# Cross-attention and 8-bit FFN on one core: both stages' quantisation factors moved from VectorE to GpSimd

## What is computed

```python
x = x + xattn(layernorm(x), ctx, mask)            # attention over 64 context rows
def _act_quant(x):                                # one factor for each row
    scale = 127.0 / clip(max(abs(x), axis=-1), 0.0001, None)
    return clip(round(x * scale), -128, 127) / scale
def _linear_bit(x, w, g):                         # w becomes ternary
    return einsum('bsd,od->bso', _act_quant(g * rmsnorm(x)), _ternary_quant(w))
n = layernorm(x)
h = silu(_linear_bit(n, w1, g1)) * _linear_bit(n, w2, g2)     # 512 -> 2048
x = x + _linear_bit(h, w3, g3)                                # 2048 -> 512
```

## Time and profile before

| what | value |
|---|---|
| median of 3 runs | 471.03 us (470.67 to 472.04) |
| the profiled execution | 472.33 us, of which the span from first to last instruction is 470.5 us |
| TensorE busy | 409.9 us (87%) |
| VectorE busy | 407.1 us (87%) |
| ScalarE busy | 339.5 us (72%) |
| GpSimd busy | 341.3 us (73%) |

### The profile page before, as it was taken

One profiled execution on the slowest core, in us unless ns is written; L12 is line 12 of the kernel. 1 busy time (PEld: TensorE's weight loads), 2 busy tenths in 40 slices (PEclk: granted clock), 3 DMA queues, 4 the chain that ended last, 5 costly groups with the idle time before them and its releaser, 6 DMA issues. The chain is left out here.

```text
span 470.5 us, 8445 instructions
## 1 busy us (share of the span) xinstructions
PE 409.9 (87%) x1966; PEld 197.5 (42%) x1966; DVE 407.1 (87%) x927; ACT 339.5 (72%) x607; POOL 341.3 (73%) x539
## 2 busy tenths in 40 slices
PE   8326644899999999999999999999999999999995
PEld 8102412344644464446434543445444634334432
DVE  3799576889899999999999999999999999999662
ACT  1585446986798769886988788878886796666552
POOL 0267858787777787788788787778777877878650
PEclk9756795899999999999999999999999999999998
DMA  7999901545557455745574466447654444444431
GB/s 270 396 366 421 312 16 22 135 90 114 139 148 173 90 114 143 179 88 115 165 178 89 111 182 163 90 111 189 139 129 111 91 88 91 86 94 91 90 69 45
DMA packets 110504, 67.45 MB, mean 143 GB/s; under 512 B 100752, under 2 KB 100880, under 8 KB 106768
## 3 DMA queue, kind: packets, MB, share of 16 engines
q1 hardware_dynamic: 110480, 67.19, 53.9%
HBM read 34.14 MB, written 8.39 MB: 90 GB/s over the span
## 5 line engine op out<-in xcount | busy, mean ns | idle before, releaser
L521 POOL TENSOR_TENSOR stageB<-stageB,g3b 128x512 f32<-128x512 f32 x128 | 163.8, 1285 | 46.2 <-DVE stageB L907 45.3
L1163 PE MATMUL S<-W2q,q12T 128*128 128x512 f16 x512 | 134.5, 386 | 8.9 <-DVE stageB L907 6.2
L1163 PE MATMUL S<-W1q,q12T 128*128 128x512 f16 x512 | 135.3, 388 | 0.0
L693 ACT ACTIVATE sg<-S,asc 128x512 f32<-128x512 f32 x128 | 87.5, 683 | 54.1 <-PE S L1163 49.3
L1191 PE MATMUL DN<-W3q,stageB 128*128 128x512 f16 x512 | 118.7, 386 | 7.3 <-DMA stageB<-stageB 7.3
L907 DVE TENSOR_TENSOR stageB<-sg,S 128x512 f32<-128x512 f32 x128 | 86.7, 677 | 19.9 <-ACT sg L693 10.5
L913 DVE TENSOR_REDUCE hm<-stageB 128x1 f32<-128x512 f32 x128 | 86.5, 677 | 0.2 <-POOL stageB L521 0.2
L1163 PEld LDWEIGHTS S<-W2q,q12T 128*128 128x128 f16 x512 | 49.5, 99 | 75.3 <-DVE stageB L907 13.9
L1191 PEld LDWEIGHTS DN<-W3q,stageB 128*128 128x128 f16 x512 | 49.8, 99 | 70.3 <-issue 10.8
L1163 PEld LDWEIGHTS S<-W1q,q12T 128*128 128x128 f16 x512 | 49.8, 100 | 66.3 <-issue 10.1
L685 ACT ACTIVATE stageB<-stageB,hf 128x1024 f16<-128x1024 f32 x64 | 69.8, 1140 | 4.8 <-DVE hf L933 4.8
(11 more groups left out here) (112 smaller groups left out, 430.7 us busy)
## 6 DMA issues: line engine op xcount, KB each, us to landing
xTs<-in_xT SPq DMA_DIRECT2D x8, 1024.0 KB, 7.0
X<-in_x SPq DMA_DIRECT2D x8, 1024.0 KB, 6.0
out_x<-X SPq DMA_DIRECT2D x32, 256.0 KB, 2.9
X<-in_w1T SPq DMA_DIRECT2D x4, 1024.0 KB, 12.5
stageB<-in_w2T SPq DMA_DIRECT2D x4, 1024.0 KB, 20.4
X<-in_w3T SPq DMA_DIRECT2D x4, 1024.0 KB, 9.2
ctxr<-in_ctx SPq DMA_DIRECT2D x16, 128.0 KB, 3.1
ctxc<-in_ctx SPq DMA_DIRECT2D x8, 128.0 KB, 3.9
```

The costliest lines, as they stand in the source:

```text
L521: nc.gpsimd.tensor_tensor(gh[q][:, part], hp[:, part], g3b[:, part], ALU.mult).then_inc(s_gh_made, 1)
L693: nc.scalar.activation(sg[n % 2][:, :], S1[n % 2][:, :], ACT.Silu, scale=asc[z][:, 0:1])\
L1163: mm = nc.tensor.matmul(bank[n % 2][:, :], q12T[q][:, i * KD + k, :], w[:, n, k, :], start=(k == 0), stop=(k == KD - 1))
```

## The change

Four things change. VectorE keeps, for each stage, the plain row maximum and one reciprocal of it: `ar = 1/am` right behind `am`, and `hr = 1/hm1` right behind `hm1`. The rest of both factors is computed on GpSimd with a minimum in place of the clip: `127 * k / max(m*k, 1e-4)` is written as a constant times `min(1e-4 / m, k)`. GpSimd also makes the scale `hsc`, which gets two buffers, while `ha` has one. In stage A the two columns of `aa` and of `af` are one instruction each, where VectorE used two.

The first part of the diff is GpSimd's new functions, the second its slot, the last two VectorE's functions and slot.

```diff
+            def stage_a_factor(t, z):
+                pool.wait_ge(s_a_am, t + 1)
+                pool.wait_ge(s_a_k, t + 1)
...
+                nc.gpsimd.tensor_scalar(aa[z][:, :], am[:, :], ak[:, :], ACT_MAX_FLOOR, ALU.mult, ALU.max)\
+                    .then_inc(s_a_max, 1)
...
+                pool.wait_ge(s_a_r, t + 1)
+                nc.gpsimd.tensor_scalar(af[:, :], ar[:, :], ACT_MAX_FLOOR, ak[:, :], ALU.mult, ALU.min).then_inc(s_a_f, 1)
             def quantize_12(t):
-                pool.wait_ge(s_a_f, 2 * (t + 1))
+                pool.wait_ge(s_a_f, t + 1)
             def stage_h_root(t, z):
...
+                nc.gpsimd.tensor_scalar(hkk[:, :], hk[:, :], asc[z][:, 1:2], QMAX * QUANTUM / ACT_MAX_FLOOR, ALU.mult, ALU.mult).then_inc(s_h_kk, 1)
+            def stage_h_factor(t):
+                pool.wait_ge(s_h_kk, t + 1)
+                pool.wait_ge(s_h_max, t + 1)
...
+                nc.gpsimd.tensor_scalar(ha[:, :], hm1[:, :], hkk[:, :], QMAX * QUANTUM, ALU.mult, ALU.max).then_inc(s_h_a, 1)
+                pool.wait_ge(s_h_r, t + 1)
...
+                nc.gpsimd.tensor_scalar(hf[:, :], hr[:, :], QMAX * QUANTUM, hkk[:, :], ALU.mult, ALU.min).then_inc(s_h_f, 1)
+            def worth_3(t, q):
...
+                nc.gpsimd.tensor_scalar(hsc[q][:, :], ha[:, :], wc[:, 2:3], ACT_MAX_FLOOR / (QMAX * QUANTUM), ALU.mult, ALU.mult).then_inc(s_h_sc, 1)
@@ GpSimd, slot @@
                     stage_h_root(t - 1, (j - 1) % NZ)
+                    stage_h_factor(t - 1)
+                    if not (first and j == 1):
+                        worth_3(t - 1, (j - 1) % 2)
                 if ahead:
                     stage_a_mean(t + 2, (j + 2) % TPB)
                 if not (last and j == TPB - 1):
+                    stage_a_factor(t + 1, (j + 1) % NZ)
                     quantize_12(t + 1)
@@ VectorE @@
             def stage_a_max(t):
...
+                dve.wait_ge(s_a_am, t + 1)
+                nc.vector.reciprocal(ar[:, :], am[:, :]).then_inc(s_a_r, 1)
             def stage_h_top(t):
...
+                nc.vector.reciprocal(hr[:, :], hm1[:, :]).then_inc(s_h_r, 1)
@@ VectorE, slot @@
                     stage_h_top(t - 1)
-                    if not early:
-                        stage_h_factor(t - 1, (j - 1) % NZ, (j - 1) % 2)
                 if ahead and not (first and j == 0):
                     stage_a_gain(t + 2)
...
-                    worth_3(t - 2, j % 2)
-                    result(t - 2)
+                    result(t - 2, j % 2)
...
-                if ahead:
-                    stage_a_factor(t + 2, (j + 2) % NZ)
```

More of the change, by code:

```diff
@@ L153, in bit_ffn_xattn @@
         hkk = sb("hkk", [P, 1])
-        ha = [sb(f"ha{i}", [P, 1]) for i in range(2)]
+        ha = sb("ha", [P, 1])
         hr = sb("hr", [P, 1])
         hf = sb("hf", [P, 1])
-        hsc = sb("hsc", [P, 1])
+        hsc = [sb(f"hsc{i}", [P, 1]) for i in range(2)]
         S1 = [ps(f"S1_{i}", [P, CH]) for i in range(2)]
@@ L879, in stage_a_max @@
                 dve.wait_ge(s_a_ga, 2 * (t + 1))
+                if later(t):
+                    dve.wait_ge(s_a_max, t)
                 nc.vector.tensor_reduce(am[:, :], ga[:, :, :], AX_X, ALU.max, apply_absolute_value=True)\
                     .then_inc(s_a_am, 1)
-            def stage_a_factor(t, q):
                 dve.wait_ge(s_a_am, t + 1)
[L886 to L899, removed]
+                if later(t):
+                    dve.wait_ge(s_a_f, t)
+                nc.vector.reciprocal(ar[:, :], am[:, :]).then_inc(s_a_r, 1)
             def gate(t, n):
@@ L918, in stage_h_top, with result @@
                 dve.wait_ge(s_gh_max, NCH * (t + 1))
+                if later(t):
+                    dve.wait_ge(s_h_a, t)
                 nc.vector.tensor_reduce(hm1[:, :], hm[:, :], AX_X, ALU.max).then_inc(s_h_max, 1)
[L921 to L925, removed]
                 dve.wait_ge(s_h_max, t + 1)
-                nc.vector.tensor_scalar(ha[q][:, :], hm1[:, :], hkk[:, :], ACT_MAX_FLOOR, ALU.mult, ALU.max).then_inc(s_h_a, 1)
-                dve.wait_ge(s_h_a, t + 1)
-                nc.vector.reciprocal(hr[:, :], ha[q][:, :]).then_inc(s_h_r, 1)
-                dve.wait_ge(s_h_r, t + 1)
                 if later(t):
-                    dve.wait_ge(s_c3_made, NHALF * t)
-                nc.vector.tensor_scalar(hf[:, :], hr[:, :], hkk[:, :], QMAX * QUANTUM, ALU.mult, ALU.mult)\
-                    .then_inc(s_h_f, 1)
-            def worth_3(t, q):
-                if later(t):
-                    dve.wait_ge(s_x2_made, t)
-                nc.vector.tensor_scalar(hsc[:, :], ha[q][:, :], wc[:, 2:3], None, ALU.mult).then_inc(s_h_sc, 1)
-            def result(t):
+                    dve.wait_ge(s_h_f, t)
+                nc.vector.reciprocal(hr[:, :], hm1[:, :]).then_inc(s_h_r, 1)
+            def result(t, q):
                 dve.wait_ge(s_down_ps, t + 1)
@@ L1053, in slot @@
                 if not early and j != 1:
-                    worth_3(t - 2, j % 2)
-                    result(t - 2)
+                    result(t - 2, j % 2)
                 if attn and j < 3:
                     stage_a_max(t + 2)
-                if first and j == 1:
-                    stage_h_factor(0, 0, 0)
                 gate(t, 2)
```

42 lines of the change are left out of this document (29 added, 13 removed).

## The result

The changed kernel took 533.83 us (median of 4 runs, 532.84 to 535.06), the kernel before 471.53 us on the same chip (4 runs, 470.67 to 472.22). The ratio is 1.132, with a 95% interval of 1.128 to 1.136: 62 us slower, where 24 were forecast.

The account below looks back on a forecast made before the run. VectorE's instruction list was taken as the period, TensorE close behind. Per slot 2.20 - 0.61 - 0.41 - 0.35 = +0.83 us, over 28 slots 23.2; with the ends +24.4 on 471.03, rounded up to 496 us; range 484 to 514.

Parts of the forecast that it names:

- the step named as the one on which the forecast rests: Each slot: `c12` now stands behind `ha`, which waits for `hm1`, so `ga` starts 2.20 us later.
- `ga`'s pair takes 1.42 us: Sign in the changed profile: a pair of `ga` takes 1.42 us everywhere, 0.35 us saved for each.
- VectorE's busy share fell: Sign in the changed profile: VectorE's busy share falls below 80% in the loop.
- the waits of `gain_3` for gates: Sign in the changed profile: GpSimd's waits for gates ahead of `gain_3` shrink.
- `ha` follows `hm1` by 0.15 us: Sign in the changed profile: `ha` follows `hm1` by 0.2 us.
- the price of the small instructions in the trip: GpSimd between `hm1` and `ga`: five small instructions 1.05 us, `af` 0.43, within a trip of 3.12 us.
- the dearest: Upper bound: each small GpSimd instruction 0.37 us from start to start, trip 3.92 us, slot +1.63, 518 us.
- The savings: VectorE per slot: stage A 0.61 us, `hsc` 0.41, `ga` pair 0.35, against `ga` 2.20 later: +0.83 us.
- the rule: VectorE and GpSimd share a port pair; the first holds it, so `ga` right behind `c12` saves 0.35 us.
- Rival 1: GpSimd itself becomes the bound: 1.6 us more in a slot against 1.8 slack; about 511 us; chance 0.22.
- `hkk` costs nothing here: In the trip: `hk` ends 2 us before `hm1`, so `hkk` is covered; otherwise 0.35 us on top.
- The ends: Outside the loop: tile 1's slot 1.0 us, the kernel's end +0.2, first tiles' weight waits nothing; batch 7's slots 0, 1 +0.83 each.

Follow-up runs that it names:

- The wait alone: Plain-copy form of the kernel before, GpSimd only waiting for `hm1` of the tile before ahead of the codes `c12`, nothing moved: 483.27 us, ratio 1.025.
- codes first: Plain-copy form of the changed kernel, with `ha`, `hf` and `hsc` moved behind `c12`, `asc` and `asq` in GpSimd's list: 509.66 us, ratio 1.082.
- both remedies: Plain-copy form of the changed kernel, `ha`, `hf`, `hsc` moved behind `c12`, `asc`, `asq`, and two `ga` buffers: 501.48 us, ratio 1.062.
- eight fillers: Plain-copy form of the kernel before, with eight small GpSimd instructions that nobody needs added behind `asq` in each slot: 485.58 us, ratio 1.024.
- stage A alone: Plain-copy form of the kernel before, with only `aa` and `af` moved to GpSimd, stage H staying on VectorE: 476.69 us, ratio 1.009.
- stage H alone: Plain-copy form of the kernel before, with only `hkk`, `ha`, `hf` and `hsc` moved to GpSimd, `aa` and `af` on VectorE: 510.39 us, ratio 1.085.

## Why the prediction was right in kind and wrong in size

**Right.** Slower, and by the step named as the one on which the forecast rests: the codes behind `hm1`. The wait alone costs 13.6 us, and the changed profile shows the round trip in every slot. `ga`'s pair takes 1.42 us, VectorE's busy share fell (40.88 of 58.25 us), the waits of `gain_3` for gates went from 29.1 us in 240 to 1.8 us in 270, and `ha` follows `hm1` by 0.15 us where GpSimd is in time.

**The step that failed: the price of the small instructions in the trip**, "5 x 0.21 = 1.05 us" and `af` 0.43. Five of them took 1.77 us, 0.28 to 0.43 from start to start, `af` to `c12` 0.57, `c12` 1.48 for 1.36 and the way back 0.21 for 0.11. The trip was 4.18 us, over the 3.12 taken and over the 3.92 that I called the dearest. I had taken 0.22 from `asq`, one instruction whose successor overlapped it. The bare price, measured in a row, is 0.26. The rest, gaps of some 0.1 us between instructions that wait for semaphores, is in the rows above; a wait for the one just before explains such a gap (0.38 for 0.26), but `hsc`, `anm` and `aa` do not wait for the one just before, and why they have it stays open. This step is 1.06 us a slot, 28 x 1.06 = 30 of the 38 us that were missed.

**The savings were right by term and lost something elsewhere.** Forecast +0.83 a slot with 3.12; with 4.18 it gives 1.89, and 2.20 were measured. In the batch of after, the softmax's subtraction (0.80 to 1.18 us) and `rval` (0.23 to 0.68 us) grew, 0.8 us a batch and 0.2 a slot, which was not in the sum. `rval` now starts while products by g3 run (326.17, of 324.32 to 326.82) and ends 0.03 us behind them; before it started 0.16 us behind their end. That such collisions took over from that of `ga` is argued from these rows and was not tested. The remaining 0.1 is where GpSimd was late for `ha`. The Trainium skill ("SBUF — State Buffer", "SBUF: two separate sides") says that the pair of ports is held by whichever instruction starts first, the other blocking for its whole length. The row of small instructions beside VectorE agrees, 0.66 us each for VectorE's 0.67; I had applied the rule to `ga` alone.

**Rival 1, GpSimd as the bound, was under-weighted and wrongly separated.** I gave its list 1.6 us a slot more, 2.2 at the dearest; it became 2.95. I read its slack as 1.8, and a little over 2.2 could be added in one place. In the changed kernel the trip decides, since GpSimd still waits 1.0 us a slot; but the list lies right under it, which codes first (+40 us), both remedies (+32) and eight fillers (+12.5) show. With both remedies, where GpSimd waits for no other engine, the time was 501.5 us, more than my 496: at the real prices of the small instructions the list alone already exceeds the forecast. At the prices that I took the list would have been shorter too, so in the main this is the same wrong term a second time. The two stages also do not add: 7.0 us for stage A alone and 40.7 for stage H alone, 61.8 together.

**"`hkk` costs nothing here"** failed in part: in the slot before the one shown, `hm1` came at 314.76 and `ha`, held by `hkk`, at 315.34, and the wait of `ga` was 4.25 us.

**The ends.** Tiles up to 3 lost 5.8 us where 1.0 and two slots of 0.83 stood in the sum; tiles 27 to 31 lost 3.7 us where two slots, 1.7, did. In tile 1's slot `ga` came 2.56 us later than the 72.96 of the earlier trace rows, where I had worked out 1.4 and taken 1.0:

```profile
75.52 1.42 DVE L922 SCALAR_TENSOR_TENSOR ga<-X,anm,g12b 128x512 f32<-128x512 f32 x2 [5.75 <-POOL c L525]
```

The small instructions ahead of its codes cost their real price there too: from the end of `hk` to the codes it is 2.56 us and was 0.25. The other four of these slots lost 1.2 to 2.0 us each; they were not taken apart.

## What to carry to other kernels

Before moving small work to the engine with slack, draw the list it lands in: if an instruction that waits for the other engine stands ahead of one for which the other engine waits, the two engines take turns, and each small instruction in between lengthens the turn, in every slot. Price each at what it costs in that place, with its gap and the other engine's tile work beside it (0.26 to 0.66 us here), never at that of one favourable row. And test the slack with instructions that nobody needs, in the very place: six were free and eight were not, where the waits alone gave 1.7 us. But look at the neighbours too, since such a filler changes what runs beside what.

## What was unexpected of the hardware

- A GpSimd instruction on 128x1 elements with a factor from memory cost 0.26 us in a row by itself, 0.38 when it waited for the one before, 0.45 with an empty instruction between, and 0.66 beside VectorE instructions with two tiles in SBUF. Reductions of one tile on VectorE left it at 0.26 (6.15 us a row).
- When `ga` moved to another place beside GpSimd's list, instructions on both engines changed (means in one batch, before to after): `ga` 0.942 to 0.752 us, GpSimd's `ak` 0.94 to 0.55 and `avk` 0.51 to 0.19, but the products by g3 1.27 to 1.39, `asq` 0.27 to 0.64 and `rval` 0.23 to 0.68.
- A VectorE instruction held up by GpSimd counts as busy: the pair of `ga` ended 1.22 us behind the end of GpSimd's product by g3 in each of the three slots looked at, whether it had started 0.46 or 0.82 us behind its start.
- 2.24 us of work a slot could be added to GpSimd's list at no cost in time, though it waited 1.7 us there, and some 0.4 us more cost 12.5 us.
